# Two layers of convolution over 8 images: how VectorE sums the eight rows of the second layer's first window

## The reference

```python
# layer 0: 3x3 convolution of the spectrum, complex weights and biases
X = rfftn(gn(x)); Y = complex_conv3x3(X, w_real, w_imag) + b
x = x + irfftn(Y)
# layer 1: 15 x 15 mean filter, zero padding
x = x + mean_filter(gn(x), 15)
```

## Time and profile before

| | us |
|---|---|
| median of 3 runs | 3395.05 |
| lowest, highest | 3383.38, 3401.74 |
| the profiled execution | 3392.79 |
| its span, first to last instruction | 3390.6 |
| DVE busy in it | 3059.3 (90%) |
| PE busy in it | 3054.2 (90%) |
| POOL busy in it | 2654.4 (78%) |

### The profile page before, as it was taken

The page is one execution under the profiler, slowest core; times in us unless marked ns, Lnnn a source line. Parts: engine busy times, 40 slices in busy tenths (PEclk is TensorE's granted clock), DMA queues, the critical chain, the costliest instruction groups (busy, mean ns, idle before and its releaser), DMA issues.

```text
span 3390.6 us, 111994 instructions
## 1 busy us (share of the span) xinstructions
PE 3054.2 (90%) x35816; PEld 1854.1 (55%) x35816; DVE 3059.3 (90%) x6034; ACT 2447.0 (72%) x4750; POOL 2654.4 (78%) x2183
## 2 busy tenths in 40 slices
PE   2189989999889999999899998999989999899986
PEld 1155555555555556555555555555555555555555
DVE  7789989999889989899898998989988999899987
ACT  2568865787658876588765886578865787658876
POOL 4069975899749987599875997579974998759986
PEclk9599999999999999999999999999999999999999
DMA  8656678666876659676696667966678666877665
GB/s 207 207 91 129 128 218 260 116 127 120 269 207 126 128 138 286 167 129 128 168 291 129 128 129 201 278 117 128 129 231 238 120 127 144 262 191 129 128 145 168
DMA packets 725097, 573.48 MB, mean 169 GB/s; under 512 B 591777, under 2 KB 667137, under 8 KB 710401
## 3 DMA queue, kind: packets, MB, share of 16 engines
q1 hardware_dynamic: 702336, 451.67, 57.3%
q10 hardware_dynamic: 22400, 117.46, 13.5%
HBM read 262.08 MB, written 148.90 MB: 121 GB/s over the span
## 4 chain that ended last, share of the span: by engine, by line
PE 45%; DVE 19%; issue 12%; SPq 8%; DMA 7%; POOL 5%; ACT 3%; ACTq 1%; DVEq 1%; POOLq 0%
PE p L621 18%; PE h_ps L531 7%; PE h_odd L531 6%; DVE ob_all L1356 6%; SPq L420 5%; DMA out<-ob_all 4%; PE p L766 4%; DVE ob_all L1272 2%; DVE bd_all L1348 2%; PE h_ps L621 2%; DVE stat L1106 2%; PE p L628 2%; POOL ob_all L1435 1%; PE p L570 1%; DMA arena<-arena 1%
## 5 line engine op out<-in xcount | busy, mean ns | idle before, releaser
L621 PE MATMUL p<-arena,bd_all 64*64 64x512 f16 x16896 | 1260.3, 380 | 27.1 <-DVE ob_all L1266 14.2
L621 PEld LDWEIGHTS p<-arena,bd_all 64*64 64x64 f16 x16896 | 558.6, 105 | 432.6 <-issue 277.9
L1432 POOL TENSOR_TENSOR ob_all<-ob_all,img 128x512 f32<-128x512 f32 x512 | 664.3, 1298 | 79.2 <-DVE ob_all L1266 74.8
L1435 POOL TENSOR_TENSOR ob_all<-ob_all 128x512 f32<-128x512 f32 x512 | 654.3, 1278 | 40.1
L885 ACT ACTIVATE img<-img,half_row (+1 forms) x1024 | 488.9, 531 | 4.7
L1266 DVE SCALAR_TENSOR_TENSOR ob_all<-p,biases,cosw 128x256 f32<-128x256 f32 x1024 | 445.5, 476 | 25.5 <-PE p L621 12.6
L1272 DVE SCALAR_TENSOR_TENSOR ob_all<-p,biases,cosw 128x256 f32<-128x256 f32 x1024 | 443.3, 474 | 0.0
L1425 POOL TENSOR_TENSOR arena<-arena 128x512 f16<-128x512 f32 x256 | 309.1, 1208 | 169.4 <-ACT arena L859 169.4
L858 ACT ACTIVATE arena<-img,sc 128x512 f16 (+1 forms) x512 | 434.4, 848 | 0.0
L1284 DVE BATCH_NORM_STATS2 stat<-img (+1 forms) x512 | 355.5, 694 | 58.5
L1356 DVE SCALAR_TENSOR_TENSOR ob_all<-p,img 128x512 f32<-128x512 f32 x512 | 347.6, 679 | 66.9 <-PE p L766 44.5
(11 more groups left out here) (210 smaller groups left out, 5465.0 us busy)
## 6 DMA issues: line engine op xcount, KB each, us to landing
out<-ob_all SPq DMA_DIRECT2D x512, 256.0 KB, 4.7
bd_all<-bd_dram SPq DMA_DIRECT2D x512, 224.0 KB, 2.6
img<-in_x ACTq DMA_DIRECT2D x168, 512.0 KB, 7.1
img<-in_x ACTq DMA_DIRECT2D x112, 256.0 KB, 5.1
img<-in_x SPq DMA_DIRECT2D x24, 512.0 KB, 25.2
arena<-img SPq DMA_DIRECT2D x24, 448.0 KB, 4.4
bd_dram<-ob_all SPq DMA_DIRECT2D x11, 768.0 KB, 3.6
arena<-arena SPq DMA_TRANSPOSE x512, 2.7
```

Of the source, the lines that this page charges most:

```text
L621: m = mm(bank[out_half * HP:(out_half + 1) * HP, :], bd[s % RB][rows, 6 * lm + (j if own else j + 1), :], part, start=opens and i3 == 0, s ...
L1432: G.tensor_tensor(q, term_row[s % 2][0], parity(img[:, t, :]), ALU.add).then_inc(first_added, 1)
L1435: G.tensor_tensor(q, q, term_row[s % 2][1], ALU.add).then_inc(q_done, 1)
```

## The change

The quarters go. `clear_head` is one memset of the whole tile, and `sum_head` adds a whole row, 128 x 512, once in every fourth slot (s = 3 and s = 7), so that iterations 1 to 4 of the loop hold 8 additions an image in place of 32. The count of operations that the loop's end waits for falls from 36 to 9. The loop bounds stay (iterations 1 to 4 with additions, 5 and 6 without).

```diff
-                HEAD_OPS = NQ * (R + 2)
+                HEAD_OPS = R + 2
+                PER_TURN = NG // 4
 
                 def clear_head():
 
-                    for q in range(NQ):
-                        V.memset(head[:, q * P:(q + 1) * P], 0.0).then_inc(head_chain, 1)
+                    V.memset(head, 0.0).then_inc(head_chain, 1)
 
                 def sum_head(i, s):
 
-                    t = (i - 1) * (NG // NQ) + s // NQ
-                    cols = slice(s % NQ * P, (s % NQ + 1) * P)
+                    t = (i - 1) * PER_TURN + s // 4
                     dve.wait_ge(x1_whole, b * T + t + 1)
-                    dve.wait_ge(head_chain, b * HEAD_OPS + (i - 1) * NG + s + 1)
-                    V.tensor_tensor(head[:, cols], head[:, cols], img[:, t, cols], ALU.add).then_inc(head_chain, 1)
+                    dve.wait_ge(head_chain, b * HEAD_OPS + t + 1)
+                    V.tensor_tensor(head, head, img[:, t, :], ALU.add).then_inc(head_chain, 1)
...
-                summed = 1 + (R + 1) * NQ // NG
+                summed = 1 + (R + 1) // PER_TURN
                 with dve.Fori(1, summed) as i:
                     for s in range(NG):
                         slot(i, s, 1)
-                        sum_head(i, s)
+                        if s % 4 == 3:
+                            sum_head(i, s)
```

## The result

| | before | after |
|---|---|---|
| median of 19 runs, us | 3392.77 | 3400.91 |
| lowest, highest | 3381.24, 3401.74 | 3392.54, 3411.7 |
| span of the profiled execution | 3390.6 | 3401.2 |

The ratio is 1.0021, 95% interval [1.0011, 1.0031]: 7 us longer (4 to 11). The forecast was 3401, a change too small to count as slower by the bound of 0.5%. It was reached from a median of three runs (3395.05) that lay 2.3 above the median of 19, with +5.7 for the change; by the medians the change is +8.1. That the level was met to 0.1 us is luck: the start was too high by about as much as the step was too small.

What follows compares the result with a forecast made beforehand. VectorE was taken to bound slots with an addition, a VectorE-TensorE circle the others. Image +0.86 for additions, -0.11 for the memset, times 8, less 0.3 hidden: +5.7, median 3395.05 to 3401; range 3384 to 3416.

Steps and rivals of the forecast that it cites:

- What bounds the slots: Slots with an addition are bound by VectorE, 3.852 us; slots without one by VectorE and TensorE waiting on each other, 3.77.
- the circle: VectorE's wave term, TensorE's step 2 load, its Hilbert transform, next wave term: 3.76 us a row, no row in store.
- The slot with a whole row: Every fourth slot: VectorE's 3.65 of other work plus 0.60 for the addition, 4.25 us.
- rival 3: The whole-row addition takes 0.70 to 0.80 beside POOL: 3407 to 3414 us; chance 0.08.
- The slot behind it: The slot after a whole-row addition takes 3.71 us, as read behind a late slot in the trace.
- The memset: One memset of 0.48 for four quarters of 0.59, in a VectorE-bound slot: 0.11 us less an image.
- The hidden 0.28: In one image a wave term already waited 0.28 for TensorE behind an addition, hiding that much; 0.3 off the sum.
- The wait at the loop's end: After iteration 4's last addition VectorE idles 0.60 us as before, so this addition costs no more than the others.
- GpSimd's hold: A whole-row addition holds up GpSimd's L1425 by 0.52 us, under VectorE's own lateness, so it adds nothing.
- VectorE's busy time: Profile sign: DVE busy time some 12 to 14 us lower while the span is not.
- Rival 2: Additions come behind a POOL instruction, each losing about 1.0 us: 3409 to 3465; chance 0.07 few lost, 0.05 most.
- Rival 1: Rows balance over four slots, so VectorE's total rules: 3381 us, chance 0.04; at POOL's floor 3396, chance 0.14.

Runs made afterwards that it cites:

- e2: Changed kernel with each addition replaced by a statistics instruction over the same row, one input in SBUF, same VectorE time: 3400.71 us.
- e3: Changed kernel with half a row (128 x 256) added in every second slot, 16 additions an image: 3392.46 us.
- e9: Kernel before, with rows 0 to 3 added by quarters in iterations 1 and 2, rows 4 to 7 by eighths in 3 to 6, signal behind the loops: ratio 0.9973.
- e4: Changed kernel with both whole-row additions of an iteration in slot s = 3, none in s = 7: 3441.16 us.
- e6: Kernel before, with the wait for the additions' end and the presummed signal moved behind the second loop (iterations 5 and 6): ratio 0.9983.
- e5: Changed kernel with the whole-row addition placed in its slot in front of low_hilbert instead of behind it: 3432.8 us.
- e7: Kernel before, with 64-column additions in all 48 slots of one loop, last two rows by quarters in the written-out slots: ratio 0.9975.

## Why the prediction was right, point by point

- **What bounds the slots.** Right. Shown: a slot above 3.77 is VectorE's own work, 3.85 with a quarter; e2 gave the same slot with GpSimd free, e3 and e9 placed slots of 3.99 and 3.79 where VectorE's sum puts them. Without an addition it is 3.77 and no later slot is shorter for an earlier one that was late (e3, e4). That the 3.77 is the circle with TensorE is read from the trace (1.77 + 1.88 + 0.11); no run changed a link of the circle.
- **The slot with a whole row**, 4.25: measured 4.26. An addition takes 0.60 from start to start beside POOL, so rival 3 (0.70 to 0.80) did not occur.
- **The slot behind it**, 3.71: mis-sized, and for a wrong reason. It is 3.76 to 3.77 after s = 3 and 3.70 after s = 7, where s = 0 takes 3.70 anyhow. In the trace of before the late slot and the first slot of a loop body coincided once an image, and I put down to the one what belongs to the other. Iteration 6 would have told them apart: it begins with no late slot in front. Eight slots cost +0.26 and not +0.18.
- **The memset**: its size right (0.485 against 0.48), its effect off: that slot gave 0.03, and the slot behind, which I held to be fixed, 0.17, since it had lost an addition too. Together -0.20 and not -0.11 an image. The two errors partly cancel: 7.8 by the slots for 5.7 forecast.
- **The hidden 0.28.** Slot 15 of the first image was 4.21 before and 4.26 after, so it was hidden there. But I read one image: in the execution before, six of eight images had lost 0.4 to 1.7 in slots 9 to 15, after it one 0.4 and one 0.5. Such losses change from execution to execution, and the sum had no term for them.
- **The wait at the loop's end** costs no more than before: right, 0.60 in both. I did not see that it was time to be had: 0.69 an image, 5.5 us, of which e6 kept about 4.
- **GpSimd's hold is covered**: right (e2). L1425 1.63 long, where "about 1.6" was forecast; the hold is 0.47 for 0.52.
- **VectorE's busy time**, 12 to 14 us lower by forecast, did not fall. The step that failed is to take a start-to-start saving as a saving in recorded busy time; it bore on no term of the sum.
- **Rival 2**, an addition behind POOL: it did not happen in the changed kernel. e4, e5 and e7, and four additions of e3, show that it is real, and where it starts: the addition has to come up while an L1425 or L1435 is under way. Its price was put at about 1.0 from one row; it is the rest of GpSimd's instruction at that moment, 1.1 in e3's four and 0.6 in e5. The Trainium skill's rule in "SBUF — State Buffer", Who interferes with whom (a VectorE instruction with two inputs from SBUF contends with a GpSimd one that reads SBUF, and order of issue decides who blocks), agrees with e4 and e5: VectorE is held with two inputs (1.25) and GpSimd by such an instruction (1.62). With one input neither is: GpSimd's L1426 behind e2's statistics took 1.17, and VectorE's L1224, which in the regular slots starts while L1435 is under way, took 0.67 to 0.69 all 512 times.
- **Rival 1**, loose coupling: fell with e3 and e4, as the late slots of the changed kernel already suggest.

## What to carry to other kernels

In this kernel, where engines hand one row round in a circle, work in excess of the circle in one slot is paid in full and idle time in the others is lost. Where you find such a circle, cut extra work into pieces as small as the idle time of each slot, even if each piece has its own fixed cost: 0.80 us of VectorE's time in four equal parts was cheaper than 0.60 in one, and 0.13 in every slot was nearly free. Count what lies over the slack, not what the engine does in all. And before taking a slot's length in a trace as the effect of what stands in front of it, look for the same slot without that.

## What the runs showed of the hardware that was not expected

- Two whole additions in a row, the second waiting for the first, let a GpSimd instruction in between them: the second took 1.41 or 1.42 instead of 0.68 in 28 of 32 places, and 1.05 to 1.28 in the others (e4). Splitting one two-input instruction into dependent ones beside a busy GpSimd can cost more than the pieces.
- Behind 1.6 us without a weight load TensorE's granted clock fell to 1.2 GHz in ten of 32 places of e4 and in four of the eight slots 2 of the changed kernel, and each fall cost 1.6 us. It was never seen to fall in these loops behind 0.64.
- GpSimd's instruction of 1.16 us, issued 0.08 behind VectorE's two-input addition of 0.60, is recorded as 1.63: the record includes the time it stands still, and shows no idle time. The hold can be seen only by comparing durations.
- The slot at s = 0 of each loop iteration takes 3.70 and the next 3.78, against 3.77 for the others, wherever they hold no addition. Why is open.
